# The late projections, the first batch's output and the first row loads at other places in three attentions of 16-wide heads

## The reference

```python
# layer 0: rotary embedding, biases, 8 key and value heads for 32 query heads
x = _layernorm(x + _L0_attn_ref(x, ...), axis=-1)
...
# layer 2: biases, 32 key and value heads, no rotary embedding
x = _layernorm(x + _L2_attn_ref(x, ...), axis=-1)
...
# layer 3: 8 key and value heads, neither bias nor rotary embedding
x = _layernorm(x + _L3_attn_ref(x, ...), axis=-1)
```

## Time and profile before

| | us |
|---|---|
| median of 3 runs (2228.36 to 2234.79) | 2234.25 |
| the profiled execution | 2234.35 |
| its span | 2232.6 |
| PE busy, DVE, ACT, POOL | 2007.4, 1110.2, 777.2, 742.5 |
| mean granted clock of TensorE | 0.947 |

### The profile page before, as it was taken

One profiled execution on the slowest core, in us unless ns is written; L12 is line 12 of the kernel. 1 busy time (PEld: TensorE's weight loads), 2 busy tenths in 40 slices (PEclk: granted clock), 3 DMA queues, 4 the chain that ended last, 5 costly groups with the idle time before them and its releaser, 6 DMA issues.

```text
span 2232.6 us, 28279 instructions
## 1 busy us (share of the span) xinstructions
PE 2007.4 (90%) x10566; PEld 1263.8 (57%) x10566; DVE 1110.2 (50%) x2019; ACT 777.2 (35%) x1649; POOL 742.5 (33%) x1199
## 2 busy tenths in 40 slices
PE   5899866999999999999998897979999788998887
PEld 2444432777777777777775685844444444544333
DVE  3656445555555555555555414135556335565344
ACT  0455523333332333333332232313565302564311
POOL 1444402534343334443332343412444202343200
PEclk9899977999999999999999897989999989999999
DMA  7222100101010101010000421134333006111100
GB/s 185 33 42 38 62 19 1 48 1 48 1 48 1 48 1 48 1 48 22 27 29 1 166 101 52 54 42 46 58 59 101 11 0 72 31 42 39 42 19 19
DMA packets 45337, 95.02 MB, mean 43 GB/s; under 512 B 7593, under 2 KB 35625, under 8 KB 41897
## 3 DMA queue, kind: packets, MB, share of 16 engines
q1 hardware_dynamic: 45202, 93.22, 16.7%
HBM read 62.20 MB, written 2.10 MB: 29 GB/s over the span
## 4 chain that ended last, share of the span: by engine, by line
PE 80%; DVE 9%; issue 4%; ACT 3%; DMA 2%; POOL 1%; SPq 1%; POOLq 0%; ACTq 0%; DVEq 0%
PE PS L1259 10%; PE PS L1328 8%; PE PS L1311 6%; PE PS L1284 6%; PE PS L535 6%; PE PS L1663 5%; PE PS L432 5%; PE PS L513 4%; PE PS L479 4%; PE PS L560 4%; PE PS L1296 3%; PE PS L1270 3%; PE PS L1674 3%; PE PS L1639 2%; PE PS L447 2%
## 5 line engine op out<-in xcount | busy, mean ns | idle before, releaser
L937 ACT ACTIVATE PB<-PS 128x512 f32<-128x512 f32 x480 | 279.4, 600 | 238.7 <-PE PS L513 235.0
L721 DVE TENSOR_REDUCE NM<-PS 128x2 f32<-128x1024 f32 x192 | 209.1, 1091 | 230.9 <-PE PS L481 229.6
L844 POOL TENSOR_SCALAR_AFFINE_SELECT PB<-PB 128x256 f32<-128x256 f32 (+1 forms) x480 | 172.7, 366 | 342.3 <-ACT PB L937 336.9
L1457 ACT COPY PRT<-PS 128x512 f32<-128x512 f32 (+3 forms) x256 | 108.8, 425 | 415.5 <-PE PS L1296 410.9
L479 PE MATMUL PS<-KQ 96*128 96x512 bf16 (+3 forms) x768 | 188.3, 310 | 30.3 <-DMA KQ<-LOW 15.9
L1417 DVE TENSOR_REDUCE NX<-PS 128x1 f32<-128x512 f32 (+3 forms) x256 | 124.1, 490 | 169.9 <-PE PS L1285 168.0
L1576 POOL TENSOR_SCALAR PR<-PR,RCP 128x512 f32<-128x512 f32 (+3 forms) x256 | 135.6, 535 | 199.7 <-DVE RCP L1405 193.4
L513 PE MATMUL PS<-KQ 99*128 99x512 bf16 (+3 forms) x768 | 184.0, 306 | 7.6 <-ACT PB L937 3.4
L1284 PE MATMUL PS<-kT,qT 128*128 128x512 f32 (+3 forms) x512 | 183.6, 440 | 4.2 <-ACT PR L1523 4.0
L432 PE MATMUL PS<-XTT,WA 128*128 128x512 f32 x288 | 149.6, 630 | 22.1 <-DMA XTT<-xT 19.3
L274 POOL TENSOR_TENSOR rstd<-ve,halfneg 128x1 f32<-128x1 f32 x64 | 44.1, 689 | 369.3 <-DVE ve L250 369.3
(11 more groups left out here) (257 smaller groups left out, 4043.5 us busy)
## 6 DMA issues: line engine op xcount, KB each, us to landing
KQ<-HI SPq DMA_DIRECT2D x108, 128.0 KB, 3.9
KQ<-MID SPq DMA_DIRECT2D x72, 128.0 KB, 4.7
WB<-f_w SPq DMA_DIRECT2D x12, 768.0 KB, 4.3
WB<-w1o SPq DMA_DIRECT2D x8, 1024.0 KB, 7.9
WC<-f_w SPq DMA_DIRECT2D x10, 768.0 KB, 4.5
WB<-w1a SPq DMA_DIRECT2D x8, 768.0 KB, 4.4
WB<-w1b SPq DMA_DIRECT2D x8, 768.0 KB, 5.9
WA<-w SPq DMA_DIRECT2D x6, 1024.0 KB, 7.6
```

What stands on the lines that cost most here:

```text
L721: x = dve.tensor_reduce(nm[:, h:h + 2, i], PS[:, b:b + 2, 0:(i + 1) * P], AX.X, ALU.max, negate=True)
L844: pool.affine_select(blocks, blocks, [[0, count], [1, P]], ALU.is_ge, 0.0, base=0, channel_multiplier=-1).then_inc(s16["probs_ready"].sem, 1)
L937: act.activation(PB[:, n % PBS, :], PS[:, 4 + n % 2, :], ACT.Exp, scale=self.scale)\
```

## The change

Five things. (1) In a0 and a3 the late chunks go to other steps ({2: 5, 3: 6, 5: 7, 7: 8, 9: 9} becomes {1: 5, 2: 6, 4: 7, 6: 8, 8: 9}) and to k = 6 to 9 in place of 1 to 4, the second batch's values from step 4, k = 1 to 4, to step 3, k = 6 to 9; what splits the chunks is moved accordingly (in a0 `turn` to a = 2 and `rotate` to k = 5 of the step behind the projection). (2) In all three the output tiles of the first batch are made at k = 7 to 9 of the same steps; `mean` comes one step later (a = 2), `root` at k = 5 of that step, `finish` (a = 2), `turn` (k = 5) and `take` (k = 5) two steps later. In a2 the last tile's `finish`, `turn` and `take` fall behind the loop. (3) The six HI loads of chunks 0 and 1 are issued by ACT, behind `high`, in place of SP. (4) `load0` waits for the first batch's XTT alone; a0 waits for the second's ahead of chunk 5. (5) SP's `load_rows` follows the table with a lag of 3 steps in a0 (was 2), 2 in a3 (was 1), 1 in a2 (as before). No matmul, copy or DMA is added or dropped.

```diff
                 self.late = {3: 8, 4: 9, 5: 10, 6: 11, 7: 12, 8: 13, 9: 14, 10: 15} if self.wide else \
-                    {2: 5, 3: 6, 5: 7, 7: 8, 9: 9}
+                    {1: 5, 2: 6, 4: 7, 6: 8, 8: 9}
+                self.lag = 1 if self.wide else 3 if rope else 2
                 self.out_step = 11 if self.wide else 10
...
                 if c == 0 and m == 5 and not self.wide:
                     pe.wait_ge(*self.aux)
+                    if self.rope:
+                        pe.wait_ge(S_xT[b].sem, 16)
                 x = pe.matmul(PS[:, self.bank(m), :], self.W[:, c, at:at + P], XTT[:, b, c, :],
                               start=(c == 0), stop=(c == NC - 1))
...
                         self.project(pe, 7, k - 5)
-                if s in self.late and 1 <= k <= 4:
-                    self.project(pe, self.late[s], k - 1)
+                first = 1 if self.wide else 6
+                if s in self.late and first <= k < first + NC:
+                    self.project(pe, self.late[s], k - first)
                 if self.wide and s in (1, 2) and 1 <= k <= 8:
                     self.project_v(pe, 1, 2 * s - 2 + (k - 1) // 4, (k - 1) % 4)
-                if not self.wide and s == 4 and 1 <= k <= 4:
+                if not self.wide and s == 3 and k >= 6:
                     for c in range(NC):
-                        self.project_v(pe, 1, k - 1, c)
+                        self.project_v(pe, 1, k - 6, c)
                 t = s - self.out_step
-                if 0 <= t < NT and 1 <= k <= 4:
-                    if k == 1:
-                        pe.wait_ge(*self.aux)
-                    x = self.out_part(pe, 0, t, k - 1, AUX)
-                    if k == 4:
+                if 0 <= t - 2 < NT and k == 5:
+                    self.turn_first(pe, t - 2)
+                if 0 <= t < NT and k >= 7:
+                    for c in ((0,), (1,), (2, 3))[k - 7]:
+                        if c == 0:
+                            pe.wait_ge(*self.aux)
+                        x = self.out_part(pe, 0, t, c, AUX)
+                    if k == 9:
                         x.then_inc(self.tails[0].s_y.sem, 1)
                         self.aux = self.tails[0].s_v.sem, self.tails[0].s_v.at(t + 1)
-                if 0 < t <= NT and k == 8:
-                    pe.wait_ge(*self.aux)
-                    self.tails[0].turn(pe, t - 1, PS[:, AUX, :])
-                    self.aux = self.tails[0].s_t.sem, self.tails[0].s_t.at(t)
+            def turn_first(self, pe, t):
+                pe.wait_ge(*self.aux)
+                self.tails[0].turn(pe, t, PS[:, AUX, :])
+                self.aux = self.tails[0].s_t.sem, self.tails[0].s_t.at(t + 1)
...
                 for part in range(3):
                     self.pv(pe, last - 1, part)
+                if self.wide:
+                    self.turn_first(pe, NT - 1)
                 self.out_part(pe, 1, 0, 2, 0)
                 self.back(pe, last - 1)
...
+                if self.wide:
+                    self.tails[0].finish(dve, NT - 1)
                 self.norm(dve, st, last - 1)
...
                 t = s - self.out_step
-                if 0 < t <= NT and a == 0:
-                    self.tails[0].finish(dve, t - 1)
-                if self.rope and a == 1 and s - 1 in self.late:
-                    self.take(dve, self.late[s - 1])
-                if self.wide and a == 2 and s in (0, 1, 2):
+                if self.rope and a == 1 and s - 2 in self.late:
+                    self.take(dve, self.late[s - 2])
+                if a == 2 and self.wide and s in (0, 1, 2):
                     self.take(dve, 6) if s == 0 else self.take_v(dve, 1, 2 * s - 2)
-                if 0 <= t < NT and a == 4:
-                    self.tails[0].mean(dve, st, t, PS[:, AUX, :])
-                if a == 5 and s in self.late:
-                    self.turn(dve, self.late[s]) if self.rope else self.take(dve, self.late[s])
-                if a == 5 and s in ((1, 2) if self.wide else (4,)):
+                if a == 2 and not self.wide and s - 1 in self.late:
+                    self.turn(dve, self.late[s - 1]) if self.rope else self.take(dve, self.late[s - 1])
+                if a == 2 and not self.wide and s == 4:
+                    self.take_v(dve, 1, 0)
+                if a == 2 and 0 <= t - 2 < NT:
+                    self.tails[0].finish(dve, t - 2)
+                if a == 2 and 0 <= t - 1 < NT:
+                    self.tails[0].mean(dve, st, t - 1, PS[:, AUX, :])
+                if a == 5 and self.wide and s in self.late:
+                    self.take(dve, self.late[s])
+                if a == 5 and self.wide and s in (1, 2):
                     self.take_v(dve, 1, 2 * s - 1)
...
                         self.causal(pool, s, k)
                         if s == 0 and k == 6 and self.wide:
                             self.low(pool, 6)
-                        if k == (5 if self.rope else 2) and s - 1 in self.late:
+                        if self.rope and k == 5 and s - 1 in self.late:
+                            self.rotate(pool, self.late[s - 1])
+                        if self.rope and k == 5 and s - 2 in self.late:
+                            self.low(pool, self.late[s - 2])
+                        if not self.rope and k == (2 if self.wide else 8) and s - 1 in self.late:
                             self.low(pool, self.late[s - 1])
+                        if k == 5 and 0 <= s - self.out_step - 1 < NT:
+                            self.tails[0].root(pool, s - self.out_step - 1)
                     if s == 0 and self.wide:
                         self.low(pool, 7)
-                    if self.rope and s in self.late:
-                        self.rotate(pool, self.late[s])
-                    if 0 <= s - self.out_step < NT:
-                        self.tails[0].root(pool, s - self.out_step)
                     b, t = divmod(s, GROUPS)
...
                 for m in range(3 if self.rope else 4):
                     self.high(act, m)
+                    if m < 2:
+                        self.high_rows(act, m)
                     self.middle(act, m)
...
                         self.exp(act, s, k)
                         if k == 1 and s >= 3 and s % 2:
                             self.take_ctx(act, (s - 3) // 2, 7)
-                        if k == 1 and s - 1 in self.late:
-                            self.high(act, self.late[s - 1]) if self.rope else self.middle(act, self.late[s - 1])
+                        if k == 1 and self.rope and s - 2 in self.late:
+                            self.high(act, self.late[s - 2])
+                        if k == 1 and not self.rope and s - 1 in self.late:
+                            self.middle(act, self.late[s - 1]) if self.wide else self.high(act, self.late[s - 1])
+                        if k == 6 and not self.rope and not self.wide and s - 1 in self.late:
+                            self.middle(act, self.late[s - 1])
                         if k == 3 and s + 1 < last:
                             self.take_max(act, s + 1)
-                        if k == 4 and self.rope and s - 1 in self.late:
-                            self.middle(act, self.late[s - 1])
+                        if k == 4 and self.rope and s - 2 in self.late:
+                            self.middle(act, self.late[s - 2])
                         if s == 0 and self.wide:
                             if k in (3, 8):
                                 self.high(act, 6 if k == 3 else 7)
                             if k in (4, 9):
                                 self.middle(act, 6 if k == 4 else 7)
-                        if k == 6 and not self.rope and s in self.late:
+                        if k == 6 and self.wide and s in self.late:
                             self.high(act, self.late[s])
+                        if k == 5 and 0 <= s - self.out_step - 2 < NT:
+                            self.tails[0].take(act, s - self.out_step - 2, PS[:, AUX, :])
                         if k == 6 and s:
                             self.take_out(act, s - 1)
-                    if 0 < s - self.out_step <= NT:
-                        self.tails[0].take(act, s - self.out_step - 1, PS[:, AUX, :])
+                if self.wide:
+                    self.tails[0].take(act, NT - 1, PS[:, AUX, :])
                 self.take_out(act, last - 1)
                 self.take_ctx(act, 2 * NC - 1, AUX)
...
+                if m >= 2:
+                    self.high_rows(sp, m)
                 rows = s16["rows%d_loaded" % (m % 3)]
-                dst = lambda r: KQ[r * HD:(r + 1) * HD, a:a + 8, :]
-                sp.wait_ge(on["hi_ready"].sem, on["hi_ready"].at(m + 1))
-                for r in (0, 1, 2) if kind == "q" else (2, 3, 4):
-                    sp.dma_start(dst(r), HI[:, m % 3, :]).then_inc(rows.sem, 16)
                 sp.wait_ge(on["mid_ready"].sem, on["mid_ready"].at(m + 1))
                 for r in (4, 5) if kind == "q" else (1, 5):
```

(21 more changed lines are left out.)

## The result

The kernel after takes 2195.43 us (median of 4 runs, 2194.56 to 2195.61); the kernel before, run on the same chip, 2231.33 (4 runs). The ratio is 0.9838, its 95% interval 0.9818 to 0.9857: faster by 1.6%, near the 2196.3 us forecast. By these medians the gain is 35.9 us (the executions of the kernel before lie between 2228.36 and 2234.79). The profiled execution took 2195.61, its span is 2193.5, 39.1 less than before's 2232.6, and on the page PE is busy for 91% in place of 90%.

What follows compares the result with a forecast made beforehand. TensorE (PE), busy 90% of the span, was taken as the bound. Gains of 7.5 (start), 21.5 (a0), 3.0 (a2), 6.0 (a3) and 0 (row loads), together 38.0, off 2234.35 gave 2196.3 us; 8 in 10 range 2180 to 2209.

Steps and rivals of the forecast that it cites:

- The start: Before a0: without the second XTT load to wait for, PE starts at about 11.75 us, not 19.28; gain 7.5 us.
- The HI loads: First scores of a0, a2, a3: ACT issuing six loads gains 0, since the busy queue, not issuing, limits them.
- the two overlapping queues: Rival, row loads of the three attentions: two queues run side by side, 13.4 us more gain, 2183 us; chance 28%.
- The excess over a3: a0's extra time for the same matmuls goes: 13.9 us in steps 3 to 10, 2.3 counted in step 14.
- The wait of scores a = 2 for maxima a = 0: a0 and a3, steps without filler at k = 1 to 4: PE waits 0.25 us in each even step.
- half of that came from `take`: a0 and a3: half of the 0.53 us wait for maxima goes, as `take` no longer stands before `norm`.
- the turn's wait for `mean`: Output tiles at k = 5, steps 12 and 13: PE stalls 0.95 us each until `mean` lets the bank go.
- the output tiles: Steps 11 to 13 of a0 and a3: 6.7 us of stall less 1.9 gives 4.8 gained in each.
- The turn behind the loop: a2: the last turn's copy stands before the copy of OT that PE's `back` waits for; costs 0.75 us.
- the late projections' move: a3: moving late projections to k = 6 to 9 gains 0.8 us, plus 0.35 in step 14.
- the new places cost more: Rival, a0 and a3, steps 2 to 13: each of about 24 steps loses 0.5 us more, 2208 us; chance 18%.
- the slower clock: Rival, a0 and a3: small waits in steps without filler let the clock fall, making it slower, 2244 us; chance 3%.

Runs made afterwards that it cites:

- e1: Kernel before with one edit: `load0` waits for the first batch's XTT alone, a0 for the second's ahead of chunk 5; 2226.26 us, ratio 0.997.
- e2: Kernel before with one edit: the HI loads of chunks 0 and 1 issued by ACT; 2233.73 us, ratio 1.0005.
- e6: Kernel after with three more 128 KB HI loads issued by ACT in each attention, which the first scores wait for; 2209.57 us (one run).
- e3: Kernel before with only part (1) of the change and its lag in `load_rows`, output tiles left in place; 2220.59 us, ratio 0.9948.
- e8: Kernel after with the first two groups of score matmuls in each step exchanged, the small one first; 2195.25 us, ratio to before 0.9832.
- e4: Kernel before with only the first batch's output tiles moved, in all three attentions; 2217.67 us, ratio 0.9937.
- e10: Kernel after plus earlier `finish`, small score group first, PE's constants wait behind its first projections, and projections filling PE's row-load wait; 2179.01 us, ratio to before 0.9763.

## Why the prediction was right

**The start.** 7.5 forecast, 7.54 measured at PE's first matmul, 7.80 (e1) and 7.91 at the first scores, 8.1 at the first `exp`. Right, with its working: released by the cast of the masks, not by the weights.

**The HI loads.** 0 forecast, 0 measured (e2), and the reason holds: a busy share of 1.13 meant that the queue, not the issuing, was the limit. e6 prices a load at 1.1 us. The rival of the two overlapping queues, which had 28%, falls.

**a0.** 21.5 forecast for the loop, 21.5 measured. Its terms stand less well than the sum, and that they meet it to a tenth is luck. The excess over a3 was the right measure (13.9 in steps 3 to 10, 2.3 in step 14): e3 alone gave 14.4 for the loop, against 13.9 + 1.2 and part of the 2.3. The wait of scores a = 2 for maxima a = 0 was mis-sized: 0.25 us in even steps was forecast, 0.48 to 0.49 measured. The step that failed is "half of that came from `take`": the wait is 1.23 us of maxima less the 0.75 us or so that PE has in between, whatever stands ahead of `norm`, and e8, which shortens the first maxima, takes some of it away. On the other side the turn's wait for `mean` was 0.47 and not 0.95, twice (the rows that the forecast names add up to 1964.46, not 1964.6, which makes 0.75); and the output tiles gave 7.8 in e4: 5.6 in steps 11 to 13, where 4.8 was forecast, 2.9 in step 14, of which I had counted 2.3 under another head, less 0.7 lost in steps 3 to 10. Errors of a microsecond each, of both signs.

**a2.** 3.0 forecast, 4.0 in the loop, 3.4 by the stages: steps 12 and 13 fell by 4.2. The turn behind the loop cost more than the 0.75 that I had put: from the end of the last `exp` to the next stage's first matmul it is 20.4 us, where it was 19.2, as the copy of OT now stands behind the turn's copy. The loop less this is 2.8. The stage gave 0.6 more ahead of the first `exp`, which no term foresaw.

**a3.** 6.0 forecast, 4.3 measured in the loop, 4.6 by the stages. e3 shows where: the late projections' move was to bring 0.8 + 0.35 there and brought -0.3. It has the same cause, 0.5 us in each even step in place of 0.25. The output part brought 4.7 of 4.8; step 12 keeps 0.35 us more than step 13, as PE waits 0.84 us for maxima there and not 0.49.

**The sum.** 38.0 forecast, 37.8 by the three stages (a0 with the start 29.8 for 29.0, a2 3.4 for 3.0, a3 4.6 for 6.0), 39.1 by the spans, 35.9 by the medians. That the errors of the stages nearly cancel is luck as well.

**Too small to matter:** a0's `max_T` waits 0.60 us for POOL in step 6, as put under "0.7 for what POOL does beside DVE"; the kernel before had waited 0.70 at that place, so nothing was lost by it. **Rivals:** "the new places cost more" was true for little over 1 us in a3 (0.8 forecast, -0.3 measured), not for the 12 us that its price would have been; the slower clock didn't come, since steps with a 0.48 us wait kept the granted clock at 1.00.

## What to carry to other kernels

Where two loops run the same matmuls at different speed, the slower one's excess is the estimate of what reordering can give, and it held within 1 us here. A small operation late in an engine's queue (here `turn`, three operations after the last maxima, and `rotate` at the end of POOL's step) costs by what stands behind it, so read the queue and not the operation. And look for what waits on a load at the end of a DMA queue: giving PE other work there took 8.4 us off a2's stage, and issuing the wanted load before the unwanted ones took 6.9 off a0's. Half a microsecond off each of many steps hardly showed in the total.

## What was unexpected of the hardware

**Two queues share the engines load by load.** Twelve loads of 128 KB into 16 partitions each land within 12.09 us, from the first to the last, from two queues (kernel after) and from one (kernel before). While both queues have loads, SP's and ACT's land in turn: ACT's at 31.46, 33.63 and 35.97 us, SP's at 30.38, 32.59 and 34.77. Three more cost 3.3 us.

**Untouched stages move by microseconds, with the half clock in them.** In the traces here the half clock comes in stretches of 3.4 to 23.9 us. With no edit near them, the stages differ from kernel to kernel: f0 took 85.2 to 88.1 us, f1 229.5 to 231.5 and f3 129.7 to 134.0, and the first `exp` of a0 up to 2.5 us earlier (e3, e4). The sum of half clock over a trace was 219.6 to 240.1 us. That the place of these stretches is what moves the untouched stages is argued from this, not tested. A gain under some 3 us is to be read from the steps it touches at clock 1.00, not from the total.

**Filling a wait doesn't always bring the clock back.** In a2 it did (1.00 for 0.92). In a0 of e10, where PE still stood 5.58 us, the granted clock was at half for 23.9 us from 35.9 on, longer than the 17.1 in two stretches of the kernel after. Why it fell for longer there isn't settled.
